# Fetching one tile in sixty-four by single-row copies from SyncE instead of a GpSimd gather, in a graph network kernel

## What is computed

```python
h = relu(layernorm(x))
x = x + L0(h)          # graph convolution: segment_sum(h[src] * norm[src], dst) * norm_dst @ W + b, relu
h = relu(layernorm(x))
x = x + L1(h)

def L1(h):                                     # one message for each edge e
    hid = relu(edge_feat @ W1 + b1)            # 32 -> 64
    w = (hid @ W2 + b2).reshape(e, 4, 8, 8)    # four 8x8 matrices for each edge
    s_e, v_e = h[src][:, :8], h[src][:, 8:].reshape(e, 8, 3)
    m0 = a * (einsum(s_e * sh0, w_000) + c * einsum(v_e, sh1, w_110))
    m1 = a * (einsum(s_e, sh1, w_011) + einsum(v_e * sh0, w_101))
    return segment_sum([m0, m1], dst) + skip(h)
```

## Time and profile before

| | before |
|---|---|
| median of the runs (three runs) | 4119.88 us (4112.54 to 4120.42) |
| span of the profiled execution, first to last instruction | 4118.7 us (the page gives no time beside the span) |
| start of layer 1's loop in SyncE's queue | 2013 us |
| last gather issued | 4090.3 us |
| POOL busy | 3083.5 us (75%) |
| PE busy | 3138.8 us (76%) |
| DVE busy | 2597.2 us (63%) |
| ACT busy | 1927.9 us (47%) |
| granted TensorE clock, mean | 0.875 of full speed |

### The profile page before, as it was taken

The page is one execution under the profiler, slowest core; times in us unless marked ns, Lnnn a source line. Parts: engine busy times, 40 slices in busy tenths (PEclk is TensorE's granted clock), DMA queues, the critical chain, the costliest instruction groups (busy, mean ns, idle before and its releaser), DMA issues.

```text
span 4118.7 us, 83555 instructions
## 1 busy us (share of the span) xinstructions
PE 3138.8 (76%) x20394; PEld 2301.4 (56%) x20395; DVE 2597.2 (63%) x5759; ACT 1927.9 (47%) x6691; POOL 3083.5 (75%) x3210
## 2 busy tenths in 40 slices
PE   5654444467777787777788888888888888888887
PEld 4544444444444443333576667666677667676676
DVE  8994333355555554454577777777777777777776
ACT  3214444443333333333655555555555555555554
POOL 7767777777777777777677777777777777777775
PEclk9996555578888888988899999999999999999998
DMA  2021111111111111111111111111111111111111
GB/s 56 14 53 40 39 39 39 39 28 23 22 23 23 23 22 21 22 22 21 27 29 29 29 29 29 28 29 30 28 28 29 29 30 29 28 28 28 30 28 18
DMA packets 244963, 119.58 MB, mean 29 GB/s; under 512 B 148880, under 2 KB 226065, under 8 KB 244817
## 3 DMA queue, kind: packets, MB, share of 16 engines
q0 software_dynamic: 102528, 52.70, 9.1%
q1 hardware_dynamic: 131625, 48.99, 5.2%
q10 hardware_dynamic: 10768, 17.44, 1.3%
HBM read 113.94 MB, written 4.92 MB: 29 GB/s over the span
## 4 chain that ended last, share of the span: by engine, by line
POOL 58%; issue 24%; DVE 9%; PE 4%; ACT 2%; DMA 2%; DVEq 2%; POOLq 1%; ACTq 0%; SPq 0%
POOL g L447 58%; DVE acc_b L970 4%; DMA g<-table,idx 1%; PE ps L756 1%; PE ps L722 1%; PE ps L790 1%; ACT onehot L554 1%; ACT acc_b L636 1%; DVEq L970 0%; DVE prod_a L1084 0%; ACT onehot L561 0%; DVE prod_a L1075 0%; DVE hn L1228 0%; DVEq L1039 0%; DVEq L1038 0%
## 5 line engine op out<-in xcount | busy, mean ns | idle before, releaser
L447 POOL DMA_INDIRECT g<-table,idx x2980 | 2868.1, 962 | 937.0 <-issue 901.4
L554 ACT ACTIVATE onehot<-iota_all,dst_rel 128x68 f32<-128x68 f32 x3320 | 845.6, 337 | 737.1 <-DVEq L1150 644.4
L846 PE MATMUL ps<-w_s,hid 128*128 128x256 f32 x3328 | 890.5, 419 | 269.2 <-ACT hid L645 221.1
L846 PEld LDWEIGHTS ps<-w_s,hid 128*128 128x128 f32 x3328 | 664.8, 208 | 438.1 <-DVE prod_a L1286 226.9
L657 ACT ACTIVATE q<-g,sh 128x32 f32<-128x32 f32 x1664 | 375.5, 308 | 867.7 <-DMA g<-table,idx 867.7
L756 PE MATMUL ps<-split_s,prod_a 128*128 128x512 bf16 x1736 | 573.9, 415 | 33.1 <-DVE prod_a L1075 31.8
L1291 DVE TENSOR_REDUCE msg_b<-prod_b 128x128 f32<-128x1024 f32 x416 | 502.9, 1209 | 0.0
L722 PE MATMUL ps<-onehot,g 128*33 128x68 f32 x2880 | 267.9, 262 | 286.5 <-issue 222.5
L1261 DVE TENSOR_TENSOR vsh<-g,sh 128x192 f32<-128x192 f32 x208 | 81.7, 393 | 587.1 <-ACT q L660 583.4
L722 PEld LDWEIGHTS ps<-onehot,prod_a 128*128 128x128 f32 x3328 | 388.8, 192 | 86.0 <-issue 85.9
L722 PEld LDWEIGHTS ps<-onehot,g 128*33 128x33 f32 x2880 | 232.1, 136 | 356.8 <-issue 330.4
(11 more groups left out here) (132 smaller groups left out, 3141.3 us busy)
## 6 DMA issues: line engine op xcount, KB each, us to landing
g<-table,idx POOLq DMA_INDIRECT x2980
ef<-edge_t SPq DMA_DIRECT2D x208, 128.0 KB
ef<-src_rows ACTq DMA_DIRECT2D x27, 512.0 KB
prod_a<-src_rows SPq DMA_DIRECT2D x124, 64.0 KB, 3.0
idx<-src_chunks SPq DMA_DIRECT2D x416, 4.0 KB
g<-x_rows,idx POOLq DMA_INDIRECT x224
sh<-sh_chunks SPq DMA_DIRECT2D x208, 16.0 KB
table<-hn ACTq DMA_DIRECT2D x5, 320.0 KB, 3.5
```

The source lines that it names most:

```text
L447: pool.indirect_dma_start(out=g[:, j, t, 0:FEAT], out_offset=None, in_=table, in_offset=bass.IndirectOffsetOnAxis(ap=idx[:, j, t:t + 1], a ...
L554: ins = act.activation(onehot[:, b, t, :], iota_all[:, 0:WIN], ACT.Square, scale=-1.0, bias=dst_rel[:, bass.ds(c * TILES + t, 1)])
L846: mm = pe.matmul(w_ps[h][:, t, :], hid[:, h, P * t:P * t + P], w2_s[:, :], start=True, stop=True)
```

## The change

The eighth tile (t = 7) of the last chunk in every eight is no longer gathered by GpSimd. SyncE fetches its 128 rows one at a time into a buffer of its own, `lone`, in `split_s`: it copies the tile's 128 source indices into one partition of SBUF (`lone_src`), loads them 20 at a time into registers, and issues for each one a DMA of one row of `table2`, 128 B, to one partition. The copies are spread over seven of the eight steps: 20 rows in each of six steps, 8 in the seventh, nothing but the list's DMA in the eighth. ScalarE copies the tile from `lone` into `g` and reads the scaled coefficients' source from `lone`. All loops of layer 1 now have 25 passes of eight chunks where they had 50 of four.

```diff
+PAIRS = ITERS // 2
+PAIR = 2 * RING
+STEP_ROWS = 20
...
+        flat_s = split_s[:, :, :, :].rearrange("p b k w -> p (b k w)")
+        lone = flat_s[:, 0:2 * FEAT].bitcast(F32)
+        lone_src = flat_s[0:1, 2 * FEAT:2 * FEAT + 2 * P].bitcast(I32)
...
-            body(0)
-            with eng.Fori(1, ITERS - 1) as i:
-                body(i)
-            body(ITERS - 1)
+            body(0, False)
+            body(1, True)
+            with eng.Fori(1, PAIRS - 1) as k:
+                body(2 * k, False)
+                body(2 * k + 1, True)
+            body(ITERS - 2, False)
+            body(ITERS - 1, True)
...
+        def has_lone(j, odd):
+            return odd and j == RING - 1
...
+            def list_lone(k):
...
+                sp.dma_start(lone_src, row).then_inc(lone_listed, 16)
+
+            def lone_rows(k, step):
+
+                if step == 0:
+                    sp.wait_ge(lone_listed, 16 * k + 16)
+                    wait(sp, coefs_ready, PAIR * k)
+                    sp.sem_inc(lone_opened, 1)
+                at = range(STEP_ROWS * step, min(P, STEP_ROWS * step + STEP_ROWS))
+                _, nodes = nc.values_load_multi_w_load_instructions(
+                    lone_src[:, at.start:at.stop], engines=[mybir.EngineType.SP], min_val=0, max_val=NODES - 1,
+                    skip_runtime_bounds_check_because="the DMA checks the address that it makes")
+                for p, node in zip(at, nodes):
+                    sp.dma_start(lone[p:p + 1, :], table2[bass.ds(node, 1), :]).then_inc(lone_in[p % 2], 16)
+
+            def lone_step(k, at):
+
+                if at == PAIR - 2:
+                    list_lone(k + 1)
+                elif at == PAIR - 1:
+                    lone_rows(k + 1, 0)
+                else:
+                    lone_rows(k, at + 1)
...
+            list_lone(0)
+            sp.wait_ge(table2_out, 16 * BLOCKS)
+            lone_rows(0, 0)
+            with sp.Fori(0, PAIRS - 1) as k:
+                for odd in (False, True):
+                    i = 2 * k + int(odd)
+                    final = final_blocks(sp, RING * i + (LOOK - 1))
+                    for j in range(RING):
+                        refill(i, j, odd)
+                        lone_step(k, RING * int(odd) + j)
+                        refill_sh(i, j)
+                    next_block(sp, blocks2, final, store)
...
-            over_iterations(pool, lambda i: gather(
-                i, table2, i + ITERS, lambda c, j: wait(pool, d_ready, c - RING + 1)))
+            over_iterations(pool, lambda i, odd: gather(
+                i, table2, i + ITERS, lambda c, j: wait(pool, d_ready, c - RING + 1),
+                lambda j: TILES - 1 if has_lone(j, odd) else TILES))
...
+                apart = has_lone(j, odd)
+                act.wait_ge(gathered[j], landed2(i, j, odd))
                 act.wait_ge(sh_in[j], 16 * (i + 1))
+                if apart:
+                    for b in range(2):
+                        act.wait_ge(lone_in[b], 4 * P * i + 4 * P)
+                    act.wait_ge(d_ready, c - RING + 1)
+                    act.activation(g[:, j, TILES - 1, 0:FEAT], lone, ACT.Copy)
```

More of the change, by code:

```diff
@@ L82, in gnn_program @@
     assert EARLY % RING == 0 and REG_ITERS > A_ITERS + 1
+    assert ITERS % 2 == 0 and STEP_ROWS * (PAIR - 1) >= P and STEP_ROWS % 4 == 0
     assert BLOCKS % TABLE_PARTS == 0
@@ L230, in gnn_program @@
         seg2_done, added2 = sem("seg2_done"), sem("added2")
+        lone_listed, lone_opened = sem("lone_listed"), sem("lone_opened")
+        lone_in = [sem(f"lone_in{b}") for b in range(2)]
         onehot2_ready, squares_made, joined2 = sem("onehot2_ready"), sem("squares_made"), sem("joined2")
@@ L317, in landed1, with landed2 @@
             return GATH * i + (first_table + GATH)
-        def landed2(i):
-            return GATH * i + (landed1(REG_ITERS - 1, True) + GATH)
+        def has_lone(j, odd):
+            return odd and j == RING - 1
+        def landed2(i, j, odd):
+            before = landed1(REG_ITERS - 1, True)
+            if j < RING - 1:
+                return GATH * i + (before + GATH)
+            return (GATH - 8) * i + (before + (GATH - 8 if odd else GATH))
         def number(i, j):
@@ L412, in store @@
                 sp.dma_start(block_rows(out, b), block_columns(xc, b)).then_inc(out_stored, 16)
[L414 to L427, removed]
+            def list_lone(k):
+                row = src_rows[PAIR * k + (PAIR - 1):PAIR * k + PAIR, CHUNK - P:] if isinstance(k, int) else \
+                    src_rows[bass.ds(PAIR * k + (PAIR - 1), 1), CHUNK - P:]
+                sp.dma_start(lone_src, row).then_inc(lone_listed, 16)
@@ new lines, in lone_step, with refill @@
+            def lone_step(k, at):
[5 more added lines that the diff above has]
+                    lone_rows(k, at + 1)
+            def refill(i, j, odd):
+                c = RING * i + j
+                sp.wait_ge(hidden_psum, 2 * c + 2)
+                sp.dma_start(ef_of(j), load_from(edge_t, c + RING)).then_inc(ef_in[j], 16)
+                sp.wait_ge(gathered[j], landed2(i, j, odd))
+                sp.dma_start(idx[:, j, :], load_from(src_chunks, c + RING)).then_inc(idx_in[j], 16)
@@ new lines, in refill_sh @@
+            def refill_sh(i, j):
+                c = RING * i + j
+                sp.wait_ge(messages_ready, c + 1)
+                sp.dma_start(sh[:, j, :, :].rearrange("p t d -> p (t d)"),
+                             load_from(sh_chunks, c + RING)).then_inc(sh_in[j], 16)
+            list_lone(0)
[10 more added lines that the diff above has]
+                    next_block(sp, blocks2, final, store)
@@ L428, in _ @@
+            final = final_blocks(sp, RING * (ITERS - 2) + (LOOK - 1))
+            for j in range(RING):
+                refill(ITERS - 2, j, False)
+                lone_step(PAIRS - 1, j)
+                refill_sh(ITERS - 2, j)
+            next_block(sp, blocks2, final, store)
+            for j in range(PAIR - 2 - RING):
+                lone_step(PAIRS - 1, RING + j)
             next_block(sp, blocks2, final_blocks(sp, RING * (ITERS - 1) + (LOOK - 1)), store)
@@ L437, in _, with gather @@
                       allow_small_or_imprecise_dtypes=True).then_inc(iota_done, 1)
-            def gather(i, table, iteration, free, tiles=TILES):
+            def gather(i, table, iteration, free, tiles=lambda j: TILES):
                 for j in range(RING):
@@ L445, in gather @@
                     pool.sem_inc(slots_opened, 1)
-                    for t in range(tiles):
+                    for t in range(tiles(j)):
                         pool.indirect_dma_start(
@@ L475, in _ @@
                 gather(i, table1, i + (EARLY_ITERS + 1), beside(i))
-            gather(A_ITERS - 1, table1, A_ITERS + EARLY_ITERS, beside(A_ITERS - 1), taken(True))
+            gather(A_ITERS - 1, table1, A_ITERS + EARLY_ITERS, beside(A_ITERS - 1), lambda j: taken(True))
             with pool.Fori(0, REG_ITERS - A_ITERS - 1) as i:
-                gather(i, table1, i + (EARLY_ITERS + 1 + A_ITERS), alone(i), taken(True))
+                gather(i, table1, i + (EARLY_ITERS + 1 + A_ITERS), alone(i), lambda j: taken(True))
             pool.wait_ge(table2_out, 16 * BLOCKS)
-            over_iterations(pool, lambda i: gather(
-                i, table2, i + ITERS, lambda c, j: wait(pool, d_ready, c - RING + 1)))
+            over_iterations(pool, lambda i, odd: gather(
+                i, table2, i + ITERS, lambda c, j: wait(pool, d_ready, c - RING + 1),
+                lambda j: TILES - 1 if has_lone(j, odd) else TILES))
         @block.scalar
@@ L637, in _, with relu @@
                                ACT.Copy).then_inc(turned_used, 1)
-            def relu(i, j, h):
+            def relu(i, j, odd, h):
                 if isinstance(i, int) and i >= ITERS:
@@ L646, in relu, with coefs @@
                                bias=b1_s[:, 0:1]).then_inc(hidden_ready, 1)
-            def coefs(i, j):
+            def coefs(i, j, odd):
                 if isinstance(i, int) and i >= ITERS:
@@ L652, in coefs, with onehots2 @@
                 c = RING * i + j
-                act.wait_ge(gathered[j], landed2(i))
+                apart = has_lone(j, odd)
+                act.wait_ge(gathered[j], landed2(i, j, odd))
                 act.wait_ge(sh_in[j], 16 * (i + 1))
+                if apart:
[3 more added lines that the diff above has]
+                    act.activation(g[:, j, TILES - 1, 0:FEAT], lone, ACT.Copy)
                 wait(act, weights_used, 2 * c - 2)
                 for t in range(TILES):
+                    rows = lone if apart and t == TILES - 1 else g[:, j, t, 0:FEAT]
                     act.activation(q[:, j % 2, t // 4, 1:5, t % 4, :],
-                                   g[:, j, t, 0:FEAT].rearrange("p (g i) -> p g i", i=MUL), ACT.Copy,
+                                   rows.rearrange("p (g i) -> p g i", i=MUL), ACT.Copy,
```

(24 more changed lines are left out.)

## The result

The changed kernel takes 4255.0 us (median of four runs, 4253.1 to 4257.3) against 4120.2 us before: ratio 1.033, 95% interval 1.032 to 1.034. It is slower by 135 us. The forecast was slower by 595 us, with a range from 4080 to 4980 us. The measured time lies inside that range and the direction was right, but the change in time was forecast more than four times too large.

What follows compares the result with a forecast made beforehand. GpSimd's gathers and their issue were taken as the bound; with the change SyncE's terms sum to 103.7 us per eight chunks against 80.8 before, 26 times, +595 us, giving 4715 us, range 4080 to 4980 us.

Steps and rivals of the forecast that it cites:

- GpSimd sets the pace before: Layer 1: GpSimd waits for nobody, a gather costs 1.263 us, and removing 26 saves 32.8 us.
- SyncE's room of 7.7 us a chunk: SyncE's queue in layer 1: its wait for finished messages, 7.7 of 10.1 us a chunk, seems free for the copies.
- the price of a row copy: SyncE's queue: 0.42 us for each copy's DMA, 0.61 us a row with its surroundings, 78.1 us for 128 rows.
- The floor is 0.333 us: SyncE's queue: every DMA to 128 partitions takes 0.333 us whatever its bytes, and those to fewer partitions are dearer.
- The rival's reason: SyncE's row copies: one row may use one of sixteen DMA engines, so 0.25 us or less; 4087 us, chance 0.18.
- The rival's point of decision: SyncE's row copies: at a DMA of about 0.25 us or less they fit and GpSimd keeps the pace.
- the loop ends: SyncE's queue: the loop end and block number, twice in eight chunks, 3.1 us.
- my other terms: SyncE's queue, eight chunks: refills 16.0, loop ends 3.1, index list 0.5, register loads 3.5, wait 2.5 us.
- Loads of registers, 0.5 us each: SyncE's queue: seven loads of 20 (once 8) registers, 3.5 us in eight chunks; 1.0 us each at 40 ns a further value.
- The longer body costs nothing: All loops: bodies twice as long, code fetching given zero, with one back-edge in eight chunks instead of two.
- 2.5 us for `coefs_ready`: SyncE's queue: the first 20 rows wait until ScalarE has used the last ones in the only buffer, 2.5 us.
- The 512 cycles for each DMA instruction: SyncE's queue: the skill's 512 sequencer cycles a DMA at 1.2 GHz, an estimated 0.427 us; total about 4740 us.

Runs made afterwards that it cites:

- e8: The changed kernel with SyncE copying no rows and GpSimd still leaving out the lone tile, whose messages are then wrong: 4087.0 us, ratio 0.991 to the kernel before.
- e7: The changed kernel with the `ef` loads issued by ScalarE instead of SyncE, all 128 row copies kept: 4092.1 us, ratio 0.993 to the kernel before.
- e9: The changed kernel with 12 of the 128 row copies of each lone tile left out, register loads kept: 4119.9 us, ratio 1.0011 to the kernel before.
- e10: The changed kernel with 24 rows a step instead of 20, the same 128 copies and 6 register loads instead of 7: 4239.4 us, ratio 1.030.
- e11: The changed kernel with every register load made twice and values of both used by the copies: 4457.2 us, ratio 1.083 to the kernel before.
- e12: The changed kernel with probe copies to 1 to 128 partitions before the first loop, apart and back to back: 4477 us, one run.
- e1: The changed kernel's longer loops with all 64 gathers on GpSimd and no row copies: ratio 1.002 to the kernel before, on a chip where that takes 6258 us.
- e6: The changed kernel with SyncE's loop in 12 passes of two pairs and one pair written out, 12 returns instead of 25: 4213.7 us, ratio 1.022.
- the first four kernels: The first four follow-up kernels, run on a chip where the kernel before takes 6258 us: ratios 1.002, 1.067, 1.050 and 1.107 to it.

## Why the prediction was wrong, point by point

- **GpSimd sets the pace before, 1.263 us a gather, 32.8 us to gain.** Right: e8 gained 33 us.
- **SyncE's room of 7.7 us a chunk is what the copies must fit into, and if they don't, SyncE becomes a serial bound.** Right, and the main finding: no wait in its queue, `idx` late at GpSimd, and e7, e9, e10 and e11 each move the time as a sum over the queue does, up and down.
- **The step that failed is the price of a row copy, 0.42 us for its DMA.** It is 0.228, so the copies cost 54.2 us in a pass and not 78.1; these 24 us a pass would be 620 us in 26. I had taken the row of the DMA with the fewest partitions that is there more than once, and read the earlier trace rows as "fewer partitions cost more". e12 splits the difference in two. Of the 0.19 us, 0.11 are the burst: those rows come from DMAs issued 0.04 us behind each other, and 32 partitions take 0.42 us so and 0.31 with a wait in front. The other 0.08 are the shape, 0.31 for 32 partitions against 0.23 for one; and a single partition takes 0.25 even back to back, so a row of the right shape would have given the price even out of a burst. The rival's reason, one engine of sixteen, fits e12 but for its 64 partitions, and I gave it 0.18.
- **"The floor is 0.333 us, which every DMA to 128 partitions takes" was misread.** The `idx` load goes to 128 partitions and stands in the earlier trace rows at 0.44. So a dearer row did not mean fewer partitions, and 0.333 was no floor: 127 partitions and one take 0.23.
- **The rival's point of decision was wrong too, in the other direction.** It said that at 0.25 us or less the change would be faster. At 0.228 it is slower, since what lies around the copies costs more than I charged: the loads 9.0 us instead of 3.5, the loop ends 5.7 instead of 3.1. With the measured 54.2 us for the copies and my other terms the sum would have been 79.8 us, or 77.3 without the wait for `coefs_ready`, against GpSimd's 79.5, and the forecast 4087 to 4094, on the wrong side. Errors of opposite sign left the direction right: that was luck.
- **Loads of registers, 0.5 us each.** 1.37 us for 20 values and 0.71 for 8, so some 0.055 us a value behind a fixed 0.27. My upper end, 1.0, was too low; "it stays one instruction" was no argument. That is 5.5 us a pass more than I charged, as much as the 5.4 by which the pass is longer than before.
- **The longer body costs nothing.** True of the engines that wait (e1, e8), false of the engine that had become the bound: a return costs SyncE 3.0 us (e6), where 0.12 us stood there before. Nor is its body twice as long, as the prediction has it: with the copies written out it went from 52 to 505 instructions. Twice as long (109, e8) costs 0.23 us; where between 109 and the 469 of e9, which stand still for 2.6 us, the price jumps was not tried. The profile's instruction queue shows code moving, 325 packets against 28 before, of which e8, with long loops and no copies, already has 176:

```profile
q14 instruction: 325, 2.66, 0.2%
```

- **2.5 us for `coefs_ready`.** Measured 0.2: ScalarE is through by the time SyncE comes to the step.
- **The 512 cycles for each DMA instruction.** The Trainium skill gives them (DMA: Bandwidth & Descriptors, its comparison of DmaMemcpy times), and with its 1.2 GHz for SyncE's sequencer (Advanced Engine Details and Errata, Clock Domains) they are an estimated 0.427 us, which seemed to support the row that I took. This case does not bear it out: 0.228 us for one row, 0.31 for 16 and 32, 0.35 for 128. The measurement decides.

What stays open is why instructions stand still on the first four kernels' chip, and why 64 partitions cost more than 32 or 128.

## What to carry to other kernels

An engine that seems to idle has only the time that its queue's waits show, and work given to it must be added up instruction by instruction, with register loads and loop returns, since in a serial queue the small terms decide: here 3% to the one side or 0.7% to the other was 6 us in 86. Take an instruction's price from a row of the same shape and spacing as where it will stand; where no row has that shape, a probe such as e12, a few copies ahead of the first loop, gives the number before anything is built on it. And when a queue is the bound, a look at what else stands in it pays more than trimming the new work: moving one refill a chunk to an engine that has just waited for the same thing turned the loss into a gain.

## What the runs showed of the hardware that was not expected

- A DMA's time on SyncE's queue grows with its shape from 0.230 us (1 or 127 partitions) over 0.272 (8) to 0.315 (16) and 0.351 (128), but is 0.472 for 64 partitions. Issued 0.04 us behind another it is 0.25 for one partition, 0.42 for 32, 0.47 and 0.60 for 64, 0.44 and 0.70 for 127, 1.21 and 0.44 for 128 (e12, two each).
- A load of 20 registers from SBUF takes 1.37 us (median), of 8 0.71, of one 0.27; a second load right behind the first 1.19 and 0.52 (20 and 8 values, e11).
- The return of SyncE's loop of 505 instructions costs 3.0 us each time (e6), and two copies of the body in a row cost it only once in two. The standstill behind the branch is 0.12 us at 52 instructions, 0.23 at 109 and 2.6 at 469, 505 and 1009 (before, e8, e9, change, e6).
